# New step orders for five engines, GpSimd's products in halves, and two PSUM copies on VectorE instead of ScalarE

## The reference

```python
xn = layernorm(x)
Q, K, V = l2norm(heads(Wq)), l2norm(heads(Wk)), heads(Wv)
cos = clip(Q @ K.T, -0.999, 0.999)
W = (1 - arccos(cos) / pi) ** 16
x = x + (W / W.sum(-1)) @ V @ Wo.T + bo            # cosine attention
x = x + softmax(q @ k.T / sqrt(8)) @ v + top2_experts(xn)
xn = layernorm(x)
x = x + causal_attention(xn) + fp4_linear(silu(fp4_linear(xn, w_gate)) * fp4_linear(xn, w_up), w_down)
```

## Time and profile before

| what | value |
|---|---|
| time, median of 3 runs | 1973.51 us (1963.91 to 1976.74) |
| profiled execution, its own time | 1969.34 us |
| its span, first to last instruction | 1967.5 us |
| busy share of the span: DVE, ACT, PE, POOL | 90%, 90%, 76%, 60% |
| mean granted TensorE clock, as a share of 2.4 GHz | 0.85 |
| DMA | 11.19 MB, 6 GB/s on average |

### The profile page before, as it was taken

How to read it: one execution, slowest core, us unless ns; L and a number is a source line. 1 busy time by engine, 2 the same in 40 slices (tenths; PEclk the granted TensorE clock), 3 DMA queues, 4 the chain that set the end, 5 groups by cost and what they waited for, 6 DMA issues and landing times.

```text
span 1967.5 us, 38505 instructions
## 1 busy us (share of the span) xinstructions
PE 1486.0 (76%) x12022; PEld 752.9 (38%) x12022; DVE 1766.3 (90%) x4009; ACT 1765.2 (90%) x1856; POOL 1182.2 (60%) x540
## 2 busy tenths in 40 slices
PE   2667787777777877777787787878777787777766
PEld 1223434333443433344343344343334434333433
DVE  5779999999999999999999999999999999999864
ACT  1299999999999999999999999899999999999893
POOL 1566666666666566566656666665667666665640
PEclk9578889889889888888978888897888889888776
DMA  1000000000000000000000000000000000000000
GB/s 42 3 4 1 6 1 6 5 6 6 6 3 3 6 5 6 6 6 0 6 6 5 6 5 6 0 6 6 5 6 5 6 0 6 6 5 6 4 3 6
DMA packets 21058, 11.19 MB, mean 6 GB/s; under 512 B 1431, under 2 KB 20953, under 8 KB 20956
## 3 DMA queue, kind: packets, MB, share of 16 engines
q1 hardware_dynamic: 20956, 10.20, 1.8%
...
## 4 chain that ended last, share of the span: by engine, by line
DVE 34%; ACT 24%; issue 22%; PE 16%; DVEq 1%; POOL 1%; SPq 0%; ACTq 0%; DMA 0%; POOLq 0%
ACT curve L578 13%; DVE nmax L880 6%; DVE curve L870 5%; ACT root L578 4%; PE psM L1037 3%; PE psM L1045 3%; DVE curve L874 3%; DVE acc L854 2%; PE psM L1190 1%; DVE stkT L866 1%; DVE xn L776 1%; ACT prob L578 1%; ACT L609 1%; PE psS L1095 1%; DVE h L454 1%
## 5 line engine op out<-in xcount | busy, mean ns | idle before, releaser
L530 POOL TENSOR_TENSOR root<-curve 128x2048 f32<-128x2048 f32 x128 | 478.7, 3740 | 453.1 <-DVE curve L874 453.1
L578 ACT ACTIVATE curve<-curve 128x2048 f32<-128x2048 f32 x384 | 718.8, 1907 | 5.5 <-POOL curve L533 2.2
L578 ACT ACTIVATE root<-root 128x2048 f32<-128x2048 f32 x256 | 484.6, 1906 | 0.0
L533 POOL TENSOR_TENSOR curve<-curve,root 128x2048 f32<-128x2048 f32 x64 | 354.5, 5562 | 64.4 <-ACT root L578 64.4
L578 ACT ACTIVATE prob<-psS 128x1024 f32<-128x1024 f32 x256 | 256.7, 1029 | 66.1 <-PE psS L1097 63.9
L874 DVE TENSOR_SCALAR curve<-psS 128x1024 f32<-128x1024 f32 x256 | 308.4, 1216 | 2.7 <-PE psS L1068 2.7
L880 DVE TENSOR_REDUCE nmax<-psS 128x4 f32<-128x1024 f32 x256 | 303.0, 1215 | 1.0 <-PE psS L1077 1.0
L566 POOL TENSOR_TENSOR stk<-qk,stk 128x512 f16<-128x512 f32 x128 | 147.8, 1164 | 76.9 <-ACT stk L578 76.6
L1045 PE MATMUL psM<-we,xnT 128*128 128x512 f32 x256 | 168.8, 747 | 0.0
L870 DVE TENSOR_TENSOR curve<-curve,root 128x2048 f32<-128x2048 f32 x64 | 162.0, 2531 | 6.1 <-ACT root L578 6.1
L1221 PE MATMUL psV<-curve,vc 128*32 128x256 f32 x2048 | 140.8, 406 | 29.8 <-ACT curve L578 25.9
...
## 6 DMA issues: line engine op xcount, KB each, us to landing
...
```

Source lines behind the costliest of these rows:

```text
L530: nc.gpsimd.tensor_tensor(root[:, two], curve[:, p, two], curve[:, p, two], ALU.mult).then_inc(s_sq, 1)
L533: nc.gpsimd.tensor_tensor(curve[:, p, two], curve[:, p, two], root[:, two], ALU.mult).then_inc(s_half[0], 1)
L578: return nc.scalar.activation(out, in_, func, **kw)
```

## The change

The five lists keep the same stages but for two copies; GpSimd's products are issued in two halves.

```diff
     "scalar": [
-        ("wln", 2, -1), ("wexp", 2, -1), ("wln", 3, -1), ("ln0", 0, 1), ("wexp", 3, -1), ("p1T", 0, -2), ("ln", 0, 0),
+        ("wexp", 3, -1), ("xnT", 0, 1), ("oC", 0, -1), ("s1e", 0, -2), ("proj", 0, 1), ("e", 0, 0), ("e", 1, 0),
...
-                two = slice(arg * 2 * UC, (arg + 1) * 2 * UC)
+                one, other = (slice((2 * arg + k) * UC, (2 * arg + k + 1) * UC) for k in range(2))
                 if stage == "sq":
...
-                    nc.gpsimd.tensor_tensor(root[:, two], curve[:, p, two], curve[:, p, two], ALU.mult).then_inc(s_sq, 1)
+                    nc.gpsimd.tensor_tensor(root[:, one], curve[:, p, one], curve[:, p, one], ALU.mult)
+                    nc.gpsimd.tensor_tensor(root[:, other], curve[:, p, other], curve[:, p, other], ALU.mult).then_inc(s_sq, 1)
                 if stage == "mul" and arg not in HALF_ON_DVE:
...
-                    nc.gpsimd.tensor_tensor(curve[:, p, two], curve[:, p, two], root[:, two], ALU.mult).then_inc(s_half[0], 1)
+                    nc.gpsimd.tensor_tensor(curve[:, p, one], curve[:, p, one], root[:, one], ALU.mult)
+                    nc.gpsimd.tensor_tensor(curve[:, p, other], curve[:, p, other], root[:, other], ALU.mult).then_inc(s_half[0], 1)
...
-                    activate(p1T[:, :, :].rearrange("p k q -> p (k q)"), bank[:, 0:3 * P], ACT.Copy).then_inc(s_p1T, 1)
...
-                    activate(xqT[:, :], bank[:, 0:T], ACT.Copy).then_inc(s_xqT, 1)
...
+                    nc.vector.tensor_copy(xqT[:, :], bank[:, 0:T]).then_inc(s_xqT, 1)
...
+                    nc.vector.tensor_copy(p1T[:, :, :].rearrange("p k q -> p (k q)"), bank[:, 0:3 * P]).then_inc(s_p1T, 1)
```

More of the change, by code:

```diff
@@ L72 @@
[L72 to L81, removed]
+        ("c", 4, 0), ("c", 5, 0), ("quanth", 3, -2), ("ln0", 0, 1), ("experts", 1, 0), ("c", 6, 0), ("rstd0", 0, 1),
@@ new lines @@
+        ("quanth", 4, -2), ("xnT", 0, 1), ("c", 7, 0), ("s1", 0, -2), ("quanth", 5, -2), ("proj", 0, 1),
+        ("p1T", 0, -2), ("quanth", 6, -2), ("proj", 1, 1), ("finc", 0, -1), ("gmax", 0, 1), ("norm", 0, 1),
+        ("ocT", 0, -1), ("o1", 0, -2), ("wo", 0, -1), ("ln1", 0, -1), ("rstd1", 0, -1), ("xn1T", 0, -1),
+        ("choose", 0, 1), ("quantx", 0, -1), ("choose", 1, 1), ("quantx", 1, -1), ("quantx", 2, -1),
+        ("quantx", 3, -1), ("quantx", 4, -1), ("quanth", 7, -2), ("newton", 0, 1), ("stackT", 0, 1), ("stackT", 1, 1),
@@ new lines @@
+        ("quantx", 5, -1), ("quanth", 8, -2), ("quantx", 6, -1), ("m", 0, 1), ("quantx", 7, -1), ("choose", 2, 1),
+        ("m", 1, 1), ("stackT", 2, 1), ("choose", 3, 1), ("quantx", 8, -1), ("m", 2, 1), ("stackT", 3, 1),
+        ("m", 3, 1), ("m", 4, 1), ("p1", 0, -1), ("xqT", 0, -1), ("c", 0, 1), ("mul", 1, 0), ("hmul", 0, -1),
+        ("m", 5, 1), ("m", 6, 1), ("c", 1, 1), ("mul", 3, 0), ("hmul", 1, -1), ("c", 2, 1), ("quanth", 0, -1),
+        ("m", 7, 1), ("choose", 4, 1), ("quanth", 1, -1), ("down", 0, -2), ("finf", 0, 0), ("maxT", 0, 1),
@@ L88 @@
-        ("e", 4, 0), ("e", 5, 0), ("ln", 3, 0), ("xn1T", 0, -1), ("e", 6, 0), ("high", 2, 1), ("e", 7, 0),
-        ("high", 3, 1), ("table", 1, 0), ("p1", 0, -1), ("sigm", 0, 0), ("sigm", 1, 0), ("xqT", 0, -1),
-        ("sigm", 2, 0), ("hT", 0, -2), ("hT", 1, -2), ("arctan", 0, 0), ("gu", 0, -1), ("sigm", 3, 0), ("oF", 0, 0),
-        ("arctan", 1, 0), ("gu", 1, -1), ("arctan", 2, 0), ("arctan", 3, 0),
+        ("wln", 2, -1), ("wexp", 1, -1), ("wexp", 2, -1), ("wln", 3, -1), ("ln0", 0, 1), ("maxT", 0, 0),
[4 rows of a table added]
@@ L92 @@
+        ("p1", 0, -1), ("sigm", 1, 0), ("sigm", 2, 0), ("gu", 0, -1), ("arctan", 0, 0), ("sigm", 3, 0),
+        ("arctan", 1, 0), ("arctan", 2, 0), ("gu", 1, -1), ("arctan", 3, 0), ("oF", 0, 0), ("table", 0, 0),
+        ("wln", 0, 0), ("wexp", 0, 0), ("wln", 1, 0),
     ],
     "gpsimd": [
-        ("fadd", 0, -1), ("sq", 2, 0), ("sq", 3, 0), ("norm", 0, 1), ("high", 0, 1), ("high", 1, 1), ("stack", 0, 1),
-        ("stack", 1, 1), ("unit", 0, 1), ("stack", 2, 1), ("stack", 3, 1), ("residual", 0, 1), ("mul", 0, 0),
@@ L96 @@
[L96 removed]
+        ("unit", 0, 0), ("stack", 2, 0), ("stack", 3, 0), ("mul", 0, -1), ("mul", 2, -1), ("sq", 0, 0),
+        ("residual", 0, 0), ("sq", 1, 0), ("sq", 2, 0), ("sq", 3, 0), ("norm", 0, 1), ("high", 0, 1), ("fadd", 0, -1),
+        ("high", 1, 1), ("stack", 0, 1), ("stack", 1, 1),
     ],
@@ L988, in run @@
                                             x2[:, :, :], ALU.add).then_inc(s_y, 1)
+                if stage == "xqT":
+                    bank, k = misc_bank(stage, 0, 0)
+                    dve.wait_ge(s_xqTp, due(s_xqTp, b))
+                    dve.wait_ge(s_gup, due(s_gup, b - 1))
+                    nc.vector.tensor_copy(xqT[:, :], bank[:, 0:T]).then_inc(s_xqT, 1)
                 if stage == "ocT":
@@ L993, in run @@
                     nc.vector.tensor_copy(ocT[:, :], bank[:, 0:T]).then_inc(s_ocT, 1)
+                if stage == "p1T":
+                    bank, k = misc_bank(stage, 0, 0)
+                    dve.wait_ge(s_p1Tp, due(s_p1Tp, b))
+                    dve.wait_ge(s_o1p, due(s_o1p, b - 1))
+                    nc.vector.tensor_copy(p1T[:, :, :].rearrange("p k q -> p (k q)"), bank[:, 0:3 * P]).then_inc(s_p1T, 1)
             steps(dve, ORDER["vector"], run)
```

24 lines of the change are left out of this document (4 added, 20 removed), and 12 rows, old and new, of the table ORDER.

## The result

The changed kernel takes 2000.59 us (median of 4 runs, 1998.10 to 2005.36), the kernel before 1974.61 (4 runs). The ratio is 1.0145, 95% interval 1.0118 to 1.0172: some 26 us slower. The forecast was 1987, the range 1942 to 2034; the time is in the range, but slower by over 1%, to which I had given 0.38. The profiled execution took 1998.10 around a span of 1996.3.

What follows compares the result with a forecast made beforehand. VectorE and ScalarE are near full; the period was costed as ScalarE's work plus waits: 54.7 + 3.5 = 58.2 us against 57.77, 13 us over 31 periods, so 1987 us on the median's scale; range 1942 to 2034.

Steps and rivals of the forecast that it cites:

- the forecast's 13 more: All periods: 58.2 us against 57.77, 0.4 more each, 13 us over 31 periods.
- place C: With place B, shared bank: ScalarE's `u1T` waits for its product right behind `hqT` 1, 1.0 us, 1.5 at lower clock.
- The wait before `prob`: ScalarE's wait before the third `e`, held on TensorE by `ocT`, 1.76 us in the long period, would be covered.
- the three waits: New ScalarE waits per period: `oCs` 1.3 us, `u1T` 1.1, `gu` 0 with the third `arctan` 0.75, weighted by clock.
- the lower level: TensorE's lower clock level, 0.5 against 1, taken for about a quarter of the time; there, 60 more us.
- 0.3 for the rest: ScalarE: 0.3 us per period left for what remains of all old waits.
- Nothing, but for the 0.2: GpSimd's halves: six more operations, 1.1 us per period, cost nothing except 0.2 on the chain to the third `arctan`.
- Which the shorter waits about pay: VectorE's two added PSUM copies: 0.8 us per period, about paid by shorter waits on GpSimd's halves.
- The condition under which I said I would be wrong: VectorE, not ScalarE, has fewer idle microseconds and lies on the chain; or the three waits exist with period under 57.
- wait for the last `e`: Rival: VectorE's `stkT` kind 2 copy waits for `e` 7, 1.5 us per period, 46 more, 2033 us; chance 0.2.
- The short period: Rival: TensorE runs `e` 2 to 5 without a hole, periods some 56.6 us, 36 less, 1951; chance 0.18.
- The halves do part: Opposing rival: VectorE gets no turn between GpSimd's halves, 0.5 us more per period, 2002 us; chance 0.07.

Runs made afterwards that it cites:

- e12_sbefore: Kernel before, with ScalarE's 16 passes over the curve (ln, sigmoid, ln, exp) on 1920 of 2048 columns; 1973.85 us, ratio 0.9988.
- e10_safter: Changed kernel, with ScalarE's 16 passes over the curve (ln, sigmoid, ln, exp) on 1920 of 2048 columns; 1997.40 us, ratio 1.0114.
- e3_u1T: Changed kernel, with ScalarE's copy `u1T` moved behind the second `sigm`; 2036.40 us, ratio 1.0303.
- e5_oC: Changed kernel, with ScalarE's copy `oCs` moved from right behind `xnT` to behind the copies of the first projection; 2006.98 us, ratio 1.0156.
- e1_split: Kernel before, old lists and copies, with GpSimd's products in halves; 1976.55 us, ratio 1.0015.
- e8_bcopies: Kernel before, old lists, with `p1T` and `xqT` copied on VectorE, behind quanth step 5 and `m` 3; 2010.25 us, ratio 1.0187.
- the corners: Eight kernels: old or new lists, each with neither, halves, copies on VectorE, or both; ratios to the kernel before from 1 to 1.0428.

## Why the prediction missed

**The steps that failed.** "I find no row for a difference in the filling and emptying and take none" cost the most: 1.0 + 11.3 us of the 15.8 that the profiled execution lies over the forecast's 13 more. The material was there. The printed order of place C has `hT` 1 and `p1` in one bank, and the end is the place where no other work covers that. I used those very rows to price the full flow and did not run the new order through the end itself. What stands there in place of nothing is 12.3: mainly 5.7 from `xn1T` to `u1T`, where `hT` waits for quanth and `p1` for `hT` in one bank, and 5.8 behind it, where the last quanth is held up by waits for TensorE.

**The base.** "I therefore cost the change as ScalarE's work plus the waits that the new lists leave it" is wrong as a mechanism. It gave 13 us for the 16.5 in the periods, which is then in part luck: e12_sbefore takes 1.4 us a period from ScalarE in the kernel before and nothing moves, and e10_safter takes 1.6 in the change for 3 us in all, within the intervals. The highest busy share didn't name the engine that decides. The Trainium skill, Perfetto Trace Analysis, section Identifying the Most-Contended Engine, has one optimize the engine with the highest occupancy first. Here that engine was ScalarE, at 95 in a hundred against VectorE's 94, and its cut, 44 us in 31 periods, gave 1 (e12_sbefore); VectorE, the second, gave 10 though it kept only 12 of its cut.

**Waits that go, waits that come.** The wait before `prob` went, and the three waits came where forecast: 0.8, 1.2 and 0.3 instead of 1.3, 1.1 and 0.75. (In the third I let the lower level delay `gu` 0 and not ScalarE, whose wait for `u1T` I had put 0.5 longer there; so 1.2 should have been some 0.7.) What I took as 0.3 for the rest is 1.3. But e3_u1T and e5_oC show that such a wait is no price: without the wait of `u1T` the time rose by 36, and the wait of `oCs` came back one operation on.

**GpSimd's halves.** "Nothing, but for the 0.2" holds in the old lists (e1_split, 1.0015). In the new ones, with the copies on VectorE, they are worth 44 us: the lists put a VectorE step under a GpSimd product in every period. I had read such meetings at `best` and did not ask which operations would have them in the new order.

**VectorE's load.** "Which the shorter waits about pay. Its 54 to 55 stay under a period of 58" is wrong: in the old lists the copies alone cost 37 us at the place they got (e8_bcopies). In the new lists, with halves, they win 24: `p1T`, copied by ScalarE, holds TensorE's second `proj` 0.8 a period longer. The condition under which I said I would be wrong came true: VectorE has the fewer idle microseconds in the 24 periods, 1393.53 - 1318.17 = 75 against 91, and more of the chain.

**The rivals.** VectorE did not wait for the last `e`: its copies of `stkT` waited 0.4 us in all the middle periods. The short period did not become the rule. The halves do part: `hqT` waits 0.8 and not 2.5.

**What stays open.** The 0.5 a period that the change adds is measured, and the corners show that the lists bring it; which dependencies form the loop that carries it was not isolated. Whether VectorE's work sets the pace of the kernel before isn't settled: its cuts there were mostly not kept, and what was kept nearly all came through. In the change it is not VectorE alone, and what limits the rest was not followed. None of the kernels beats the one before with its work whole.
